# Running sums of a gated attention stage made token-major, their quotients turned afterwards

## The reference

```python
    qkv = _rms(x) @ w_qkv.T
    q, k, v = jnp.split(qkv, 3, axis=-1)
    q = _rms(q)
    k = _rms(k)
    w = jnp.exp(k)
    kv_cum = jnp.cumsum(w * v, axis=1)
    w_cum = jnp.cumsum(w, axis=1)
    y = jax.nn.sigmoid(q) * (kv_cum / (w_cum + 1e-06))
    uv = y @ w_swiglu.T
    u, g = jnp.split(uv, 2, axis=-1)
    return x + u * jax.nn.silu(g) @ w_out.T
```

## Time and profile before

| | |
|---|---|
| median of three runs | 1392.12 us (1390.97 to 1394.84) |
| profiled execution, its own time | 1392.23 us |
| its span, first to last instruction | 1390.5 us |
| PE busy | 1340.8 us, 96% of the span |
| DVE busy | 819.9 us, 59% |
| ACT busy | 606.6 us, 44% |
| POOL busy | 513.0 us, 37% |
| first stage, to the MLP's first matmul on PE | 188.84 us |

### The profile page before, as it was taken

The page is one execution under the profiler, slowest core; times in us unless marked ns, Lnnn a source line. Parts: engine busy times, 40 slices in busy tenths (PEclk is TensorE's granted clock), DMA queues, the critical chain, the costliest instruction groups (busy, mean ns, idle before and its releaser), DMA issues.

```text
span 1390.5 us, 23678 instructions
## 1 busy us (share of the span) xinstructions
PE 1340.8 (96%) x8180; PEld 1068.0 (77%) x8180; DVE 819.9 (59%) x2085; ACT 606.6 (44%) x1135; POOL 513.0 (37%) x485
## 2 busy tenths in 40 slices
PE   8999999999999999999999999999988999999994
PEld 6788888888888888888886777777766877766762
DVE  5888865333333333333467787788786586666661
ACT  4444441111111111111126777777786324777772
POOL 4555542202020202020427554446453112655552
PEclk9999999999999999999999999999999999999997
DMA  6000002010110101010100000000011924566553
GB/s 257 1 0 0 0 30 107 0 46 5 42 38 8 45 0 45 0 46 1 49 12 17 21 21 21 21 5 17 6 47 46 374 81 159 92 106 105 95 98 46
DMA packets 20533, 73.41 MB, mean 53 GB/s; under 512 B 2320, under 2 KB 3344, under 8 KB 18000
## 3 DMA queue, kind: packets, MB, share of 16 engines
q1 hardware_dynamic: 10256, 46.93, 9.3%
q0 software_dynamic: 10176, 25.17, 9.2%
HBM read 52.95 MB, written 19.14 MB: 52 GB/s over the span
## 4 chain that ended last, share of the span: by engine, by line
PE 86%; DVE 6%; ACT 4%; issue 2%; DMA 1%; POOL 1%; POOLq 0%; DVEq 0%; SPq 0%; ACTq 0%
PE ps L782 21%; PE ps L784 21%; PE ps L783 21%; PE ps L1030 5%; PE ps L1215 5%; PE ps L1022 2%; DVE den L1641 2%; ACT cols L1434 2%; PE ps L1054 2%; PE ps L1122 2%; PE ps L1048 1%; ACT cols L1422 1%; PE ps L1185 1%; PE ps L1143 1%; PE ps L1019 1%
## 5 line engine op out<-in xcount | busy, mean ns | idle before, releaser
L782 PE MATMUL ps<-feat,wsplit 128*128 128x512 f32 (+1 forms) x672 | 247.1, 368 | 3.2 <-PE ps L784 2.1
L784 PE MATMUL ps<-feat,wsplit 128*128 128x512 f32 (+1 forms) x672 | 244.6, 364 | 0.0
L783 PE MATMUL ps<-feat,wsplit 128*128 128x512 f32 (+1 forms) x672 | 244.5, 364 | 0.0
L1291 ACT ACTIVATE sg<-ps 128x512 f32<-128x512 f32 x64 | 38.3, 598 | 369.1 <-PE ps L784 369.0
L1561 DVE TENSOR_TENSOR m_f<-ps,sg 128x512 f32<-128x512 f32 x64 | 44.2, 691 | 245.4 <-ACT sg L1291 245.4
L542 POOL CAST wsplit<-wraw 128x3072 fp32r<-128x3072 f32 x9 | 24.8, 2755 | 399.3 <-PEq L970 386.7
L1829 DVE CUSTOM_DVE_ANT_0 cols<-ps,msk 128x256 f32<-128x256 f32 (+1 forms) x512 | 146.2, 353 | 27.7 <-PE ps L1022 16.3
L782 PEld LDWEIGHTS ps<-feat,wsplit 128*128 128x128 f32 x672 | 126.7, 189 | 26.4 <-issue 6.6
L1422 ACT COPY cols<-ps 128x512 f32<-128x512 f32 x192 | 111.6, 581 | 77.7 <-PE ps L1030 77.7
L784 PEld LDWEIGHTS ps<-feat,wsplit 128*128 128x128 f32 x672 | 126.6, 188 | 19.9
L783 PEld LDWEIGHTS ps<-feat,wsplit 128*128 128x128 f32 x672 | 126.7, 189 | 19.7
(11 more groups left out here) (281 smaller groups left out, 3014.5 us busy)
## 6 DMA issues: line engine op xcount, KB each, us to landing
wraw<-weights SPq DMA_DIRECT2D x11, 1536.0 KB, 6.5
rawx<-weights SPq DMA_DIRECT2D x8, 1536.0 KB, 16.1
ctx_raw<-ctx_t SPq DMA_DIRECT2D x8, 512.0 KB, 4.6
h_rows<-hd POOLq DMA_DIRECT2D x16, 256.0 KB, 4.4
out<-acc SPq DMA_DIRECT2D x4, 1024.0 KB, 4.7
qkv_raw<-weights SPq DMA_DIRECT2D x6, 512.0 KB, 7.5
acc<-x SPq DMA_DIRECT2D x1, 3072.0 KB, 17.5
acc<-x SPq DMA_DIRECT2D x2, 512.0 KB, 7.0
```

What stands on the lines that cost most here:

```text
L782: nc.tensor.matmul(out_, w_hi, m_hi, start=first, stop=False)
L783: nc.tensor.matmul(out_, w_lo, m_hi, start=False, stop=False)
L784: return nc.tensor.matmul(out_, w_hi, m_lo, start=False, stop=last)
```

## The change

The running sums are made token-major: `scan(b, pb, tt)` takes one tile of 128 tokens over all 512 features, with the triangle (and for the second tile a square of ones for the first tile's tokens) as the loaded operand and w or w times v as the moving one. The first tile takes four matmuls of 512 columns, the second eight. The four transposes of exp(−q) per half are gone, and so is ACT's `w_cum`; in their place ACT adds 1 to each tile of exp(−q) in place (semaphore `e1`), and DVE adds the 1e-6 in the first step of `y_a`. The quotient, now token-major in `den` with a place per tile, is turned by PE (`turn_y`) one projection later, for the second tile in the next batch, and `y_hi` and `y_lo` read it from PSUM bank 6. ACT's second tile of exp(−q) waits for DVE's denominators (`den`) in place of PE's scan, and so does the load of the second weight slot. Batches 1 and 6 are written out beside the loop, since the late turn starts at batch 2.

```diff
-            def scan(b, pb, half):
+            def scan(b, pb, tt):
...
                 for bank, kind in ((5, 0), (4, 1)):
+                    terms = [(t, part) for t in range(tt + 1) for part in range(2)]
+                    for n, (t, part) in enumerate(terms):
+                        ones = tri[:, 0:P] if t == tt else tri[:, P:2 * P]
+                        mm = nc.tensor.matmul(ps[:, bank, :], ones, wv_s[:, place_a(pb, t), kind, part, :], start=(n == 0), stop=(n == len(terms) - 1))
+                mm.then_inc(a["scan"], 1)
+
+            def turn_y(b, tt):
+
+                pe.wait_ge(a["y"], 2 * b + tt + 1)
+                after(pe, a["yT"], 2 * b + tt)
+                for k in range(KB):
+                    tr = nc.tensor.transpose(ps[:, 6, k * P:(k + 1) * P], den[:, tt, k * P:(k + 1) * P], ident[:, :])
+                tr.then_inc(a["yT_ps"], 1)
...
+            def batch_a(b, pb, first, last, late=True):
                 project(b, 0, 0)
+                if late:
+                    turn_y(b - 2, 1)
                 project(b, 0, 1)
                 transposes(b, 1)
                 if not first:
                     scan(b - 1, 1 - pb, 0)
...
                 project(b, 1, 1)
+                if not first:
+                    turn_y(b - 1, 0)
                 project(b, 1, 2)
...
                 if tt == 1:
-                    after(act, a["scan"], 2 * b)
+                    after(act, a["den"], 2 * b)
...
+                act.wait_ge(a["e"], t + 1)
+                nc.scalar.activation(e_t, e_t, ACT.Copy, bias=1.0).then_inc(a["e1"], 1)
...
-                exp_k(b, pb, 0, None if first else lambda: w_cum(b - 1, 0))
-                if not first:
-                    y_hi(b - 1, 0)
+                exp_k(b, pb, 0)
...
                 if not first:
-                    y_hi(b - 1, 1)
+                    y_hi(b - 1, 0)
                 wv_hi(b, pb, 1)
...
+                nc.vector.scalar_tensor_tensor(out=den[:, tt, :], in0=ps[:, 5, :], scalar=1e-6, in1=e_q[:, place_a(pb, tt), :], op0=ALU.add,
                                                op1=ALU.mult).then_inc(a["den"], 1)
...
+                if late:
+                    y_lo(b - 2, 1)
                 hT_lo(b, 1)
                 if not first:
-                    y_a(b - 1, 0)
+                    y_a(b - 1, 1 - pb, 0)
...
                     hT_lo(b + 1, 0)
-                if not first:
-                    y_lo(b - 1, 0)
-                if not last:
                     h_a(b + 1, 1)
                 if not first:
-                    y_a(b - 1, 1)
+                    y_a(b - 1, 1 - pb, 1)
+                    y_lo(b - 1, 0)
                 w_times_v(b, 1)
-                if not first:
-                    y_lo(b - 1, 1)
-                    dve.wait_ge(a["yT"], 2 * b)
```

More of the change, by code:

```diff
@@ L381, in decoder_layer @@
             w_hi_piece="pieces of w_qkv with hi", w_piece="pieces split", w2_hi="parts of the first MLP slot with hi", w2="parts split", shift="batches whose residual's scale and shift are made",
-            w_sum="running sums of w, half batches", scan="those of w * v and exp(-q)^T too", wce="w's sums plus 1e-6",
-            den="denominators", rec="their reciprocals", y="outputs, half batches", yhi="their hi in feat", yT="their lo too",
+            scan="tiles with the running sums of w and of w * v", e1="tiles of 1 + exp(-q)",
+            den="denominators", rec="their reciprocals", y="tiles of outputs", yT_ps="transposed in PSUM", yhi="their hi in feat", yT="their lo too",
             pool="GpSimd's own small steps", dve="the vector engine's")
@@ L845, in project @@
                 mm.then_inc(a[name], 1)
-            def scan(b, pb, half):
-                s = 2 * b + half
-                if half == 0:
+            def scan(b, pb, tt):
+                if tt == 0:
                     pe.wait_ge(a["split"], 2 * b + 2)
-                    pe.wait_ge(a["e"], 2 * b + 2)
                 else:
-                    pe.wait_ge(a["y"], s)
-                at0, at1 = place_a(pb, 0), place_a(pb, 1)
+                    pe.wait_ge(a["y"], 2 * b + 1)
                 for bank, kind in ((5, 0), (4, 1)):
[L858 to L872, removed]
@@ L960, in steps @@
                                     pe.wait_ge(a["yT"], 4 * (s + 2))
-                                up(s + 1, npar, nch, nch == 0, turn + 1, False)
+                                up(s + 1, npar, nch, nch == 0, turn + 1, False, meanwhile if isinstance(s, int) and s == 0 else None)
                                 if isinstance(s, int) and s == 0:
@@ L1322, in exp_q @@
                 act.wait_ge(a["rms"], 2 * t + 1)
-                nc.scalar.activation(e_q[:, place_a(pb, tt), :], ps[:, 1, :], ACT.Exp, scale=rq[:, 0:1]).then_inc(a["e"], 1)
+                nc.scalar.activation(e_t, ps[:, 1, :], ACT.Exp, scale=rq[:, 0:1]).then_inc(a["e"], 1)
+                act.wait_ge(a["e"], t + 1)
+                nc.scalar.activation(e_t, e_t, ACT.Copy, bias=1.0).then_inc(a["e1"], 1)
             def exp_k(b, pb, tt, between=None):
@@ L1339, in wv_hi, with y_hi, batch_a @@
                 nc.scalar.copy(wv_s[:, place_a(pb, tt), 1, 0, :], wv_f[:, :]).then_inc(a["wv_hi"], 1)
[L1341 to L1353, removed]
+            def y_hi(b, tt):
+                act.wait_ge(a["yT_ps"], 2 * b + tt + 1)
+                at_ = b * SEQ + tt * P
+                cols = slice(at_, at_ + P) if isinstance(b, int) else bass.ds(at_, P)
+                nc.scalar.copy(feat[:, 0, :, cols], ps[:, 6, :].rearrange("p (k n) -> p k n", k=KB)).then_inc(a["yhi"], 1)
+            def batch_a(b, pb, first, last, late=True):
+                exp_q(b, pb, 0, (lambda: y_hi(b - 2, 1)) if late else None)
                 hT_hi(b, 1)
-                exp_k(b, pb, 0, None if first else lambda: w_cum(b - 1, 0))
-                if not first:
-                    y_hi(b - 1, 0)
+                exp_k(b, pb, 0)
                 wv_hi(b, pb, 0)
@@ L1360, in batch_a @@
                     hT_hi(b + 1, 0)
[L1361 to L1366, removed]
+                exp_q(b, pb, 1, (lambda: first_hi(0)) if last else None)
                 exp_k(b, pb, 1, (lambda: first_hi(1)) if last else None)
                 if not first:
-                    y_hi(b - 1, 1)
+                    y_hi(b - 1, 0)
                 wv_hi(b, pb, 1)
@@ L1385, in _ @@
                 nc.scalar.copy(wsplit[:, s, 0, at_:at_ + PIECE_A], qkv_raw[:, n * PIECE_A:(n + 1) * PIECE_A]).then_inc(a["w_hi_piece"], 1)
[L1386 to L1387 removed]
+            batch_a(0, 0, True, False, False)
+            batch_a(1, 1, False, False, False)
+            with act.Fori(0, BATCH // 2 - 2) as i:
                 for r in range(2):
[L1389 removed]
+                    batch_a(2 * i + (2 + r), r, False, False)
+            batch_a(BATCH - 2, 0, False, False)
             batch_a(BATCH - 1, (BATCH - 1) % 2, False, True)
             first_hi(JB)
[L1393 to L1394 removed]
             step = mlp_act(act, mlp)
+            y_hi(BATCH - 2, 1)
             step(0, 0, True)
[L1398 to L1399 removed]
+            for tt in range(TPB):
+                y_hi(BATCH - 1, tt)
             for s in range(1, 2 * CHUNKS):
```

67 lines of the change are left out of this document (38 added, 29 removed).

## The result

The changed kernel takes **1405.94 us** (median of four runs, 1404.3 to 1406.67) against 1392.45 for the kernel before (median of four): a ratio of 1.0094, 95% interval 1.0079 to 1.0108. It is slower by 0.9%, 13.5 us. The profiled execution took 1406.41 us, its span 1404.7, which is 14.2 longer than before.

The account below looks back on a forecast made before the run. A loop of waits round all engines, not PE's work, was taken as the bound. Start 0.7, five periods 11.0 and tail 5.8 sum to 17.5: span 1390.5 becomes 1408.0, forecast 1410.0 us, range 1398 to 1419.

Parts of the forecast that it names:

- PE's saved 8.2 us: PE's scans and turns: 1.03 us less work per batch, 8.2 in eight, counted 0 in the five periods.
- The loop's period, 24.9: Loop of waits through all engines, once per batch: 24.9 us in place of 22.66, +2.2; five periods +11.0.
- The split takes 1.28 to 1.74; I take 1.5: POOL's split of the second tile's w times v: 1.5 us taken, ending at 15.0 in place of 12.42.
- I take 3.15: DVE's denominator of the second tile starts 3.15 us after the loop's zero, from a range of 2.96 to 3.66.
- The estimate of 3.29: Same denominator by the skill's exclusive port lock: 2.71 + 0.54 + 0.04 = 3.29, the sum 0.7 us higher over five batches.
- I take 0.95: Length of DVE's `ha` of the first tile, closing the loop: 0.95 us from a range of 0.54 to 1.35.
- PE's clock falls: Rival: new waits throttle PE's clock, delaying the denominator about 1.4 us; +8.5 on the forecast, 1418, chance 0.10.
- The tail, +5.8: Batch 7 and the MLP's first steps, with waits for late outputs: +5.8 us, from +4 to +7.5.
- The start, +0.7: Batches 0 and 1: the new copy comes twice before the first `ha`, the scan wait goes: +0.7 us.
- PE's waits, over 2 us for `ha` and about 1.1 at the late turn: PE stands still some 4 us per batch, for `ha` and at the late turn, which waits for `y_lo`.
- y_lo is met early: Rival: only the new copies and the denominator's wait count, +0.5 us per period and half the tail: 1398, chance 0.12.

Follow-up runs that it names:

- k4: Changed kernel with twelve needless PE transposes per batch ahead of the turn of the next batch's first tile: 1405.86 us (1.0098).
- k12: Kernel before, with only PE's second scan of the last batch moved ahead of the turn of the next batch's first tile: 1391.42 us (0.999).
- k10: k5 plus DVE's residual update ahead of `y_lo`, PE's second scan ahead of the next first tile's turn, its denominator ahead of that tile's low half: 1383.05 us (0.9924).
- k2: Changed kernel with `y_hi` moved ahead of the exp of k on ACT: 1397.19 us (1.0038).
- k3: Changed kernel with both ACT copies 1 + exp(−q) moved behind the square of k: 1402.21 us (1.0071).
- k5: Changed kernel with both ACT edits, those of k2 and k3, together: 1391.40 us (0.9987).
- k1: Changed kernel with w times v of the second tile moved ahead of `y_lo` on DVE: 1402.84 us (1.0086).
- k7: Changed kernel with DVE's denominator of the last batch's second tile ahead of `ha` of the next batch's second tile: 1404.92 us (1.0087).

## Why the prediction was right, and where its sizes were off

The sign, the mechanism and the range held: 1405.9 against a forecast of 1410.0 and a range of 1398 to 1419. By its steps:

- **PE's saved 8.2 us count 0 in the periods:** held. k4 puts 1.1 us a batch back on PE and the time does not move. The saving itself, 1.03 a batch, is 1.04 between k12's busy time and k10's.
- **The loop's period, 24.9:** too long. Measured 23.86 to 23.99 where the clock held. This term of the sum was mis-sized, +2.2 a period where clean ones gave +1.3. Step by step from `ha`'s end: denominator 2.94 (said 3.15), square 3.65 (3.88), exp of k 9.21 (9.45), `y_lo` 11.23 (11.37), w times v 11.84 (11.98), split 13.36 (13.50), exp of the next q 16.09 (16.69), low half 17.94 (18.58), `ha` 23.26 (23.92), and it takes 0.73 (0.95). The chain and its order are as forecast; three terms make the 0.9.
- **"The split takes 1.28 to 1.74; I take 1.5":** it took 1.30, and the scale behind it 1.43 (112.53 to 113.96) where I had carried over 1.69 from before. The old 1.74 ran beside `y_lo` of 1.27 and the residual update; the change itself moves them away, which I did not follow. Together 0.46.
- **The denominator, "I take 3.15":** 0.21 too late. `ha` at 100.25 began beside the split (99.30 to 100.60) and ended at 100.88, 0.28 behind its end, and the denominator began 0.07 before that. Every `ha` that met a split under way shows this 0.28 (last section); with it the split's end at 2.71 gives 2.92, and 2.94 was measured. The Trainium skill, "SBUF — State Buffer", section "SBUF: two separate sides", has the ports that VectorE and GpSimd share locked for the whole of whichever instruction starts first, the other fully blocked, and these rows agree. The estimate of 3.29 in the prediction was too late all the same, because it put the full 0.54 of `ha` behind the split, where only 0.28 was left.
- **`ha`, "I take 0.95":** 0.63 to 0.73 in the clean periods, since POOL's split of w had only 0.35 to 0.45 left when `ha` began.
- **PE's clock falls (0.10):** it did, behind two of the five waits, to 0.63 and 0.58, and those periods were 24.80 and 25.15: some 2 us, not the 8.5 of that rival.
- **The tail, +5.8:** +5.0. The MLP's first turn waited 3.45 (said 3.7), the scan before it 1.10 (1.9), the last output's turn 0.99 (1.2).
- **The start, +0.7:** 0.76 by the same count; the other 1.25 is this execution's own.
- **PE's waits, over 2 us for `ha` and about 1.1 at the late turn:** 1.66 to 1.82 and 0.79 to 0.84 in the clean periods (2.20 and 2.02, and 0.50, in the others), some 2.5 a batch where the prediction had 4. The loop is 0.9 shorter, and PE's own work 21.0 (k10) and not 20.8.
- **The rival "y_lo is met early", 1398:** it did not come by itself, and k2, which makes it so, took 1397.2. That mechanism was priced right.

Shown by undoing: `y_lo`'s wait, with its tail, 9 us (k2); the copies 4 (k3); both together the whole loss (k5). Single edits gave less than they shorten on DVE's chain, because the residual updates then met POOL's splits (k1, k2) and `ha` ended behind POOL's split (k1, k3). The square's wait for the denominator was not removed by itself: it would take a fourth place for exp(−q), for which that region has no room.

## What to carry to other kernels

Before crediting saved work on the busiest engine, look at that engine's own waits at the same step of each period: if it stands still once per period for another engine, a loop sets the time, and the saved work is worth nothing until the loop is shorter than the work. Price each moved step by what stands behind it on its queue, here w times v behind `y_lo` behind an exp. Look for the second path into the same step: `ha` ended behind POOL's split as well as behind DVE's chain, so two single edits (k1, k3) gave back half of what they shortened. Then ask which order makes the loop fall below the work: the same change lost 0.9% as it was ordered and gained 0.8% with a few steps moved.

## What the runs showed of the hardware that I had not expected

- An `ha` (DVE, from SBUF to SBUF) that met one of POOL's splits ended 0.27 to 0.30 us behind the end of that split, however much of the split was still to run; it took 0.59 to 1.59 by that. So it was in all 144 rows of the fourteen traces in which the split had begun before it or at most 0.04 behind; the 79 that met none took 0.53 to 0.55. Once DVE began first, by 0.10 us (k12, 68.21): `ha` took 0.54 and the split 1.58 in place of 1.28. The two residual updates took 0.99 us clear of the splits and 1.09 to 3.11 beside them. `y_lo` before, which reads SBUF alone, ended 0.54 to 0.56 behind a split; `y_lo` now, with an operand in PSUM, took 0.69 beside a split as elsewhere. The kernel before, POOL and then DVE's `ha` of the earlier trace rows (112.65 + 1.35 = 114.00, 0.28 behind 113.72):

```profile
112.43 1.29 POOL L603 TENSOR_TENSOR wv_s<-w_k,wv_s 128x512 fp32r<-128x512 f32 x1 [1.69 <-ACT wv_s L1335]
```

- PE's clock fell to 0.63 and 0.58 behind waits of 2.20 and 2.02 us in one execution and stayed at 1.00 behind 2.21 and 2.00 in another (k7, the rows below). The length of the wait alone does not decide it; what does stays open.

```profile
47.10:51.10 4.00, 4.00 (x20) 3.39 (x21) 2.67 (x4) 1.79 (x4) 1.29 (x1) 1.00 0.01 2
70.80:74.80 4.00, 4.00 (x20) 3.38 (x21) 2.66 (x4) 1.79 (x4) 1.30 (x1) 1.00 0.00 0
```
